# Two attention layers on one core: the attention matmuls of a tile in one block, three tiles of lookahead, row sums closed in a chunk's last step, GpSimd work in halves

## The reference

```
# layer 0
q, k, v = Wq x + bq, Wk x + bk, Wv x + bv             # 32, 32 and 256 channels
x = gamma0 * v softmax(q^T k, over the queries i) + x   # attn[i, j], out[:, j]
# layer 1
theta = theta_w x + theta_b                            # 32 channels, 4096 positions
phi, g = maxpool2(phi_w x + phi_b), maxpool2(g_w x + g_b)   # 32 and 128 channels, 1024 positions
y = gamma1 * (out_w (g softmax(theta^T phi)^T) + out_b) + x
```

## Time and profile before

| | us |
|---|---|
| median of 3 runs | 2871.97 (2869.93 to 2874.7) |
| the profiled execution | 2867.3 |
| its span in the trace | 2865.5 |
| first tile begun, exponentials | 72.9 |

### The profile page before, as it was taken

How to read it: one execution, slowest core, us unless ns; L and a number is a source line. 1 busy time by engine, 2 the same in 40 slices (tenths; PEclk the granted TensorE clock), 3 DMA queues, 4 the chain that set the end, 5 groups by cost and what they waited for, 6 DMA issues and landing times.

```text
span 2865.5 us, 39235 instructions
## 1 busy us (share of the span) xinstructions
PE 2707.4 (94%) x12260; PEld 2159.1 (75%) x12260; DVE 2003.4 (70%) x3303; ACT 1743.5 (61%) x3171; POOL 1945.4 (68%) x1480
## 2 busy tenths in 40 slices
PE   6999999989999999998999999999889999999988
PEld 5777777766687777776678777777667777777766
DVE  7677677767767777776766777776676777777665
ACT  5556555556755565566665655556566555555666
POOL 2676766657767666665686666667477666666768
PEclk9999999999999999999999999999899999999999
DMA  2000000011200000001121000000112000000011
GB/s 84 1 23 16 23 15 16 15 38 64 70 30 20 19 16 16 15 16 44 60 74 31 15 16 15 16 15 16 45 59 73 16 16 16 15 16 16 15 45 59
DMA packets 43193, 85.02 MB, mean 30 GB/s; under 512 B 2672, under 2 KB 2800, under 8 KB 42992
## 3 DMA queue, kind: packets, MB, share of 16 engines
q1 hardware_dynamic: 35360, 68.17, 7.0%
q10 hardware_dynamic: 7632, 14.36, 1.7%
HBM read 48.96 MB, written 33.55 MB: 29 GB/s over the span
## 4 chain that ended last, share of the span: by engine, by line
PE 66%; issue 14%; POOL 11%; ACT 7%; DVE 2%; DMA 0%; POOLq 0%; ACTq 0%
PE o_ps L826 27%; PE o_ps L805 14%; PE s_ps L795 7%; POOL prob_l L442 7%; PE aux L863 7%; POOL xa L462 3%; PE aux L837 2%; ACT prob_h L505 2%; PE aux L872 2%; PE aux L880 1%; PE aux L841 1%; ACT prob L502 1%; PE aux L876 1%; ACT queries L527 1%; ACT psums L524 1%
## 5 line engine op out<-in xcount | busy, mean ns | idle before, releaser
L442 POOL TENSOR_TENSOR prob_l<-prob,prob_h 128x512 fp32r<-128x512 f32 x1280 | 1636.2, 1288 | 727.3 <-ACT prob_h L505 723.4
L502 ACT ACTIVATE prob<-s_ps 128x512 f32<-128x512 f32 x1280 | 767.8, 600 | 947.2 <-PE s_ps L795 945.5
L672 DVE TENSOR_REDUCE mx<-aux 128x1 f32<-128x512 f32 x1103 | 760.2, 689 | 447.7 <-PE aux L863 445.7
L826 PE MATMUL o_ps<-prob_h,vh 128*128 128x512 f32 x2304 | 936.3, 406 | 13.3 <-issue 12.6
L826 PE MATMUL o_ps<-prob_h,vl 128*128 128x512 f32 x2304 | 904.2, 392 | 0.0
L634 DVE TENSOR_TENSOR acc<-prob,acc 128x512 f32<-128x512 f32 x1216 | 836.4, 688 | 47.7 <-ACT prob L502 37.8
L805 PE MATMUL o_ps<-prob_l,vh 128*128 128x512 f32 x2304 | 755.4, 400 | 47.0 <-POOL prob_l L442 46.9
L505 ACT ACTIVATE prob_h<-s_ps 128x512 fp32r<-128x512 f32 x1280 | 762.8, 596 | 0.0
L805 PEld LDWEIGHTS o_ps<-prob_l,vh 128*128 128x128 f32 x2304 | 436.4, 191 | 158.2 <-POOL prob_l L442 70.7
L826 PEld LDWEIGHTS o_ps<-prob_h,vh 128*128 128x128 f32 x2304 | 436.7, 190 | 120.1 <-issue 26.2
L795 PE MATMUL s_ps<-queries,keys 128*128 128x512 f32 x1280 | 507.8, 398 | 8.0 <-DVE vl L650 6.5
(11 more groups left out here) (122 smaller groups left out, 1970.9 us busy)
## 6 DMA issues: line engine op xcount, KB each, us to landing
xa<-x SPq DMA_DIRECT2D x32, 512.0 KB, 3.6
spill<-xa SPq DMA_DIRECT2D x32, 512.0 KB, 2.7
xa<-spill SPq DMA_DIRECT2D x32, 512.0 KB, 3.7
y<-xa SPq DMA_DIRECT2D x32, 512.0 KB, 2.8
xp<-x ACTq DMA_DIRECT2D x26, 512.0 KB, 3.8
xp<-x SPq DMA_DIRECT2D x2, 512.0 KB, 9.3
prob<-w_in ACTq DMA_DIRECT2D x1, 576.0 KB, 5.4
wo<-w_out ACTq DMA_DIRECT2D x1, 128.0 KB, 6.1
```

What stands on the lines that cost most here:

```text
L442: nc.gpsimd.tensor_tensor(out=prob_l[:, i, :], in0=prob[:, i, :], in1=prob_h[:, i, :].bitcast(f32), op=ALU.subtract).then_inc(pl_ready, 1)
L502: nc.scalar.activation(prob[:, i, :], s_ps[s][:, :], ACT.Exp).then_inc(p_ready, 1)
L672: ins = nc.vector.tensor_reduce(out=dst, in_=bank[:, :], axis=AX.X, op=ALU.max)
L826: last = mm(o_ps[ct][:, :], value(parts, l, t, ct), prob_h[:, h % RING, :], start=t == 0 and parts is vh, stop=False)
```

## The change

1. `av_low` and `av_high` become one function, `attend`: for each channel half vh with `prob_h`, vh with `prob_l`, vl with `prob_h`, all at tile g. The stationary operand vh stands twice in a row. The wait for POOL's `prob_l` is now in the middle of the tile to which it belongs, where it was one tile later. One semaphore, `av_done`, takes the place of `av_h` and `av_l`.
2. PE and ACT run three tiles ahead (`AHEAD` 3), POOL and DVE two (`SPLIT_AHEAD`, `SUM_AHEAD`). The rings keep their sizes.
3. `copy_acc` runs one tile earlier, and `D1` in the chunk's last tile (place 2) instead of the next chunk's first; `D2` follows in that first tile instead of the third.
4. POOL's subtraction for `X` (now `XL`) and its addition `N` are cut into halves of 512 columns at tiles of their own; K1 waits for each half by itself. `XB` is moved into its chunk's tile 22.
5. In layer 1 many jobs move to other tiles and banks; `Z`, `ZA` and the maxima mostly to place 3. The last two chunks' `V0` of the next image (four jobs, two before) are done in that image's layer 0. The list before layer 1 has `D1` and one `V0` fewer.

```
-AHEAD = 2
+AHEAD, SPLIT_AHEAD, SUM_AHEAD = 3, 2, 2
...
-                put(g, 1, on(Job("D1", *prev, 0), X1))
-                put(g + 2, 1, on(Job("D2", *prev, 0), X1))
+                put(g, 1, on(Job("D2", *prev, 0), X1))
                 if prev[0] == 0:
                     c = prev[2]
-                    put(g + 1, 1, Job("XB", *prev, 0))
-                    put(g + 3, 1, Job("N", *prev, 0))
-                    put(g + 6, 1, Job("X", 1, b, c, 0))
+                    put(g + 1, 1, Job("N", *prev, 0))
+                    put(g + 3, 1, Job("N", *prev, 1))
+                    put(g + 5, 1, Job("X", 1, b, c, 0))
+                    put(g + 6, 1, Job("XL", 1, b, c, 0))
+                    put(g + 8, 1, Job("XL", 1, b, c, 1))
...
+            put(g + 22, 1, Job("XB", 0, b, n, 0))
...
+            put(g + KT[0] - 1, 2, on(Job("D1", 0, b, n, 0), X1))
...
             before[tile_no(1, b, 0)] = [
-                d1, k0, d2, v00, add, v01, rnd, k0l, v00l, v01l, k1_, v10, k1_l, v10l, v11, v11l,
-                k1, Job("X", 0, b + 1, 2, 0), k1k, g1, k1m, t1, *st, k2, m0, k1q, k1l, t1l, v20, k2l, v20l, v21, v21l,
-                Job("X", 0, b + 1, 3, 0)]
+                d2, k0, v00, *add, v01, *rnd, k0l, v00l, v01l, k1_, v10, k1_l, v10l, v11, v11l,
+                k1, *rounding(0, b + 1, 2), k1k, g1, k1m, t1, *rounding(0, b + 1, 3), *st, k2, v20, m0,
+                k1q, k1l, t1l, k2l, v20l]
...
                 for k in range(CT):
-                    put(g + 4 + 2 * k, 1, on(Job("Z", *prev, k), X0))
-                    put(g + 5 + 2 * k, 1, Job("ZA", *prev, k))
+                    put(g + 2 + 2 * k, 3, on(Job("Z", *prev, k), X0))
+                    put(g + 3 + 2 * k, 3, Job("ZA", *prev, k))
...
+            put(g + KT[1] - 1, 2, on(Job("D1", 1, b, n, 0), X0))
...
-                if t == KT[l] - 1:
+                if t == KT[l] - SUM_AHEAD:
                     copy_acc(l, b, n)
...
-                for parts in (vh, vl):
-                    last = mm(o_ps[ct][:, :], value(parts, l, t, ct), prob_h[:, h % RING, :],
-                              start=t == 0 and parts is vh, stop=False)
+                i = h % RING
+                mm(o_ps[ct][:, :], value(vh, l, t, ct), prob_h[:, i, :], start=t == 0, stop=False)
+                if ct == 0:
+                    pe.wait_ge(pl_ready, h + 1)
+                mm(o_ps[ct][:, :], value(vh, l, t, ct), prob_l[:, i, :], start=False, stop=False)
+                last = mm(o_ps[ct][:, :], value(vl, l, t, ct), prob_h[:, i, :], start=False, stop=t == KT[l] - 1)
                 if ct == VT[l] - 1:
-                    last.then_inc(av_h, 1)
+                    last.then_inc(av_done, 1)
...
-                if g:
-                    av_low(g - 1)
                 for job in BEFORE.get(g, ()):
                     entry(job)
+                fresh = g in BEFORE
                 for h in begun_at(g, AHEAD):
-                    scores(h)
+                    if not (fresh and h == g + SRING):
+                        scores(h)
                 entries_at(1)
-                av_high(g, 0)
+                attend(g, 0)
                 entries_at(2)
                 if VT[l] > 1:
-                    av_high(g, 1)
+                    attend(g, 1)
+                if fresh:
+                    scores(g + SRING)
                 entries_at(3)
```

More of the change, by code:

```diff
@@ L108, in project0, with rounding @@
                 on(Job("V0", 0, b, c, 1), v1), Job("V0L", 0, b, c, 1))
+    def rounding(l, b, c):
+        return [Job("X", l, b, c, 0)] + [Job("XL", l, b, c, k) for k in range(CT)]
     def put(g, place, *jobs):
@@ L115, in make_plan @@
     st_turn = [X0, O0, A]
-    begin = [Job("X", 0, 0, 0, 0), Job("X", 0, 0, 1, 0)]
+    begin = [*rounding(0, 0, 0), *rounding(0, 0, 1)]
     for c in range(NCH):
@@ L121, in make_plan @@
         if c + 2 < NCH:
-            begin.append(Job("X", 0, 0, c + 2, 0))
+            begin += rounding(0, 0, c + 2)
     begin += [maxima(0, 0, 0, NCH - 1, s, (X0, O0, A, X1)[s]) for s in range(SUBS)]
@@ L169, in make_plan @@
         m0 = on(Job("M", 1, b, 0, 0), X1)
-        add, rnd = Job("N", *last, 0), Job("X", 1, b, c, 0)
+        add = [Job("N", *last, k) for k in range(CT)]
+        rnd = rounding(1, b, c)
         k1k, k1q, k1m, k1l = (Job(name, 1, b, c, 0) for name in ("K1K", "K1Q", "K1M", "K1L"))
@@ L206, in make_plan @@
                 if n < NCH - 1:
-                    for s, (t, place, at) in enumerate(((0, 1, X1), (2, 3, Y), (3, 3, Y), (4, 1, X1))):
+                    for s, (t, place, at) in enumerate(((2, 3, Y), (3, 3, Y), (5, 3, X0), (6, 3, X0))):
                         put(g + t, place, maxima(0, b + 1, 0, n, s, at))
@@ L440, in split_prob @@
                 pool.wait_ge(ph_ready, h + 1)
-                wait(pool, av_l, h - RING + 1)
+                wait(pool, av_done, h - RING + 1)
                 nc.gpsimd.tensor_tensor(out=prob_l[:, i, :], in0=prob[:, i, :], in1=prob_h[:, i, :].bitcast(f32),
@@ L456, in entry @@
                     pool.wait_ge(xb_ready, CT * image0(b, c) + CT)
[L457 to L463 removed]
+                    if k == 0:
+                        pool.wait_ge(normed, image0(b, c) + 1)
+                    else:
+                        wait_free(pool, Job("D2", 0, b, c, 0))
+                    nc.gpsimd.tensor_tensor(out=xa[slot][:, k, :], in0=osb[:, k, :], in1=xa[slot][:, k, :],
+                                            op=ALU.add).then_inc(x1_ready, 1)
                 elif name == "ZA":
@@ L473, in _ @@
                     entry(job)
-                for h in begun_at(g, 1):
+                for h in begun_at(g, SPLIT_AHEAD):
                     split_prob(h)
@@ L764, in _ @@
                     entry(job)
-                fresh = t == KT[l] - 1
+                fresh = t == KT[l] - SUM_AHEAD
                 if not fresh:
-                    for h in begun_at(g, 1):
+                    for h in begun_at(g, SUM_AHEAD):
                         add_prob(h)
@@ L799, in value, with attend @@
                 return parts[l][:, t, ct * P:(ct + 1) * P]
-            def av_low(h):
-                l, b, n, t = tile_at(h)
-                pe.wait_ge(pl_ready, h + 1)
-                for ct in range(VT[l]):
-                    last = mm(o_ps[ct][:, :], value(vh, l, t, ct), prob_l[:, h % RING, :],
-                              start=False, stop=t == KT[l] - 1)
-                last.then_inc(av_l, 1)
-            def av_high(h, ct):
+            def attend(h, ct):
                 l, b, n, t = tile_at(h)
```

108 lines of the change are left out of this document (48 added, 60 removed).

## The result

The changed kernel takes 2784.6 us (median of four runs, 2783.2 to 2787.2) against 2871.6 (2869.9 to 2874.7): a ratio of 0.9697, 95% interval 0.968 to 0.9714. That is 87 us faster where 143 were forecast. The time is inside the range, but it is the time of rival (a), layer 1 gaining nothing (2785), and not that of the forecast (2729).

What follows compares the result with a forecast made beforehand. PE's work plus its pauses was taken as the bound. Gains of 74 (layer 0), 51 (layer 1), 5 (last image), 11.5 (list before layer 1) and 1 (beginning) sum to 142.5 us, giving 2729 us, range 2670 to 2800.

Steps and rivals of the forecast that it cites:

- rival (a): Layer 1 gains nothing, as POOL, ACT and DVE do the same work per tile there; 2785 us, chance 0.14.
- What bounds the kernel: Whole kernel: PE, busy for 94% of the span, sets the time by its work plus its pauses.
- Same values twice running: Attention matmuls: the second use of vh in a row is no cheaper; gain taken as 0.
- Lookahead: Layer 0: the prob_l wait goes, 1.16 us per chunk; with D1, 2.3 taken per chunk, -74 us over 32 chunks.
- rival (c): Slower: the prob_l wait before the next scores delays the whole ring, baring POOL's halves; 2891 us, chance 0.10.
- D1 earlier: Layer 0's chunk changes: the waits before D1 and the next chunk's first matmul both go, 0.9 us per chunk.
- Covered by 0.9 us of matmuls: D2's new wait for the reciprocal is hidden by 0.9 us of matmuls between D1 and D2.
- Halves: Layer 0: POOL's pieces become halves of 1.2 us, no longer waiting for xh, against 3.1 us of cushion.
- Layer 1: Images with projections: 17 of 22 to 30 us gained per image, three times, -51 us (0 to -75).
- The list before layer 1: Net 3 us per image, three times, plus 2.5 before the last layer 1: -11.5 us (+3 to -18).
- Rival (d): No change to speak of: layer 1 gains nothing and half of the slower case comes; 2872 us, chance 0.04.
- The marks of the profile after: Expected signs: layer 0 chunks 64.1 us, prob_l and psums waits under 10, layer 1 some 130, PEclk near 1.0, DVE above 74%.

Runs made afterwards that it cites:

- e1: Changed kernel with each channel half's last two attention matmuls exchanged, so no stationary operand stands twice in a row: 2788.1 us, ratio 0.9703.
- e2: Changed kernel with the earlier lookahead (PE and ACT two tiles ahead, POOL one), all else as changed: 2896.7 us, ratio 1.0081.
- e6: Kernel before with only the attention matmuls of a tile put in one block, the prob_l wait mid-tile: 2964.5 us, ratio 1.032.
- e4: Changed kernel with row-sum copy, D1 and D2 back in their old places, N, X, Z later, DVE sums one tile ahead: 2846.7 us, ratio 0.9902.
- e3: Changed kernel with both halves of XL and of N back to back on POOL at the first one's place: 2789.8 us, ratio 0.9705.
- e5: Changed kernel with layer 1's old banks and places and the old list ahead of it, without D1 there: 2808.8 us, ratio 0.978.
- the runs with a light DVE: Changed kernel, layer 1's maxima and row sums on half the columns: 2763.8 us; with ACT's exponentials halved too: 2751.8 us.

## Why the prediction was right or wrong

**What bounds the kernel: right.** PE's work plus PE's pauses; PE's work did not change, and the gain is the pauses.

**Same values twice running, 0: right** (spacing 0.23 either way; e1). The weight load of the second use is issued all the same.

**Lookahead, layer 0: right in kind, 14 us too much of 74.** The wait for prob_l is 1.3 us in all, and 66.4 became 64.3, where 64.1 was forecast: with 2.1 of its 2.6 us of pauses gone the 2.1 named was the whole of it, and the added 0.2 for small ones was too much, 6 us in all. The other 8 are in the first chunk of each image. That of the first image, which follows no other chunk, gained 0.3 us for 2.1. Those of images 2 to 4 take 69.7, 69.8 and 68.4 us, where the 66.5 of before, less 2.1 and with 2.8 of moved V0, would be 67.2. In them D1 waits 0.51 us and D2 0.45 (second image) or 0.82 (fourth), and the granted clock of the first 10 us is 0.83 in the two slower ones and 1.00 in the fourth. The prediction priced every chunk alike. The lookahead's price (e2, 110 us) is above anything it said, and the one-go attention alone loses 92 (e6), for which it has no term outside rival (c): the sum hid two large terms of opposite sign in one of 1.16 us per chunk.

**D1 earlier: right.** 0.9 us per chunk forecast, 1.0 by e4. "Covered by 0.9 us of matmuls" holds for D2 in layer 0; in layer 1, where DVE has maxima in its queue, D2 waits 0.8 us in two places, and D1 still waits 2.0 us for psums once.

**Halves: said to be needed for the cushion, they are not** (e3). The prediction's own account says so: 3.1 us of cushion is more than the 2.6 of a whole piece.

**Layer 1: the step that failed.** "I take 17 of 22 to 30 per image"; measured are, without the moved V0, 1.5 per image in the first two and 8.5 in the third, 11.5 against 51 in all. Four things are wrong in it. It took the named pauses (D1, prob_l) as ended and the rest as shortened; they did end, 14.4 us of PE's idle time became 10.3, but others came behind them, and DVE ends most of the new ones (4.2 of the 5.9 us). Nor did the third tile shorten the rest by itself: in the old places layer 1 gains nothing (e5), and its small gain came with the new places, which have no term in the sum. It weighed DVE by its share, 84% of a stage of 129, and called that room; the runs with a light DVE show that DVE at 110 of 144 us already costs 4 to 8 us per image. The waits name single maxima and queries that come late, which a mean doesn't show; that this is the reason is argued, not shown, since the light runs cut load and steps together. It took DVE's 36 waits for psums for a sign of DVE being late in layer 1, as rival (a) did, but 31 of them are at the start of chunks of layer 0, and the second image's layer 1 has one, of 3.0 us. And it booked the 7 us of slow clock as part of what goes, "PEclk near 1.0"; the clock was lost in the wait at the entry, which grew from 2.38 to 3.55 us, and in one that the change brought, for the second chunk's queries, and the granted clock is 0.94. Rival (a) had the mechanism ("POOL, ACT and DVE there do for each tile what they did") and 14%; it was the nearest, and its time, 2785, is the time measured, but that is luck: layer 1 gave 14 us where rival (a) has nothing, and layer 0 and the list gave 18 less than it has them.

**The list before layer 1: -7.9 for -11.5**, inside its bounds. The 2.38 us before the scores were to go because the banks are free early. In the second image three scores instead of two need three banks, and the third is T1's, whose rest DVE computes late: 3.55 us. What was taken as ended is a new wait for the same kind of work. Before the last layer 1, where the prediction took 2.5 us, nothing was gained: PE's waits there, 4.67, 2.57 and 0.79 us for xh, nm_wide and the queries, are 4.65, 2.57 and 0.79 after the change.

**The third rival (c)** is not what happened, but e6 shows its mechanism and sign at lookahead two. Its point of decision, 2.8 us of other work in one loop, was not measured with three tiles; 2.6 us of POOL back to back (e3) don't reach it, and one tile less (e2) is the difference between 0.97 and 1.008. Rival (d)'s 2872 doesn't follow from its words: (a)'s 2785 and half of the 162 us between (c) and the forecast are 2866.

**The marks of the profile after:** chunk 64.3 for 64.1; PE's waits for prob_l and psums 1.3 + 8.0, under 10 as said; scores 1.84 apart; layer 1 of the second image 144 for 130; clock 0.94 for 1.0; DVE 72%, not above 74 (2004 us of work in the forecast's span of 2723 would have been 73.6%).

## What to carry to other kernels

Where a stage is a ring over four engines, do not book its pauses and its low clock as won when the largest named wait goes. Ask what the next engine in the round has in its queue at that moment, and when its results come, beside its share of the time. A structural edit and the lookahead that pays for it are two terms: price each alone, since their sum hides that one is negative. Look at the entry of a stage: deeper lookahead asks for its buffers and its inputs earlier, so whatever feeds the first tiles has to move up with it.
